# Four weight sums moved from ScalarE to VectorE in a cross-attention and feed-forward kernel

## The reference

```python
def attention(ctx, latents, mask):            # latents = layernorm(x)
    xn, ln = layernorm(ctx), layernorm(latents)
    q = ln @ W_q                               # 4 heads of 64
    k, v = split(concat([xn @ W_kv, ln @ W_kv]))
    sim = (rmsnorm(q) * 64**-0.5) @ rmsnorm(k).T
    return softmax(where(mask, sim, -max)) @ v @ W_out + b_out

def bit_linear(x, w):                          # both sides quantized
    sx = 127 / clip(max|x| over the row, 1e-5);   xq = clip(round(x * sx), -128, 127) / sx
    sw = 1 / clip(mean(|w|), 1e-5);               wq = clip(round(w * sw), -1, 1) / sw
    return xq @ wq.T

x = x + attention(ctx, layernorm(x), mask)
h = bit_linear(layernorm(x), w1)               # 256 -> 1024
h = silu(depthwise_conv3_over_tokens(h) + conv_b)
x = x + bit_linear(h, w2)                      # 1024 -> 256
```

## Time and profile before

| | us |
|---|---|
| median of 3 runs | 440.35 (440.3 to 441.3) |
| profiled execution, its own time | 440.35 |
| its span, first to last instruction | 438.5 |
| TensorE busy | 407.9 (93%) |
| VectorE busy | 379.5 (87%) |
| ScalarE busy | 314.4 (72%) |

### The profile page before, as it was taken

How to read it: one execution, slowest core, us unless ns; L and a number is a source line. 1 busy time by engine, 2 the same in 40 slices (tenths; PEclk the granted TensorE clock), 3 DMA queues, 4 the chain that set the end, 5 groups by cost and what they waited for, 6 DMA issues and landing times.

```text
span 438.5 us, 14218 instructions
## 1 busy us (share of the span) xinstructions
PE 407.9 (93%) x5918; PEld 276.6 (63%) x5918; DVE 379.5 (87%) x611; ACT 314.4 (72%) x368; POOL 84.3 (19%) x119
## 2 busy tenths in 40 slices
PE   1999997699999999999999999999999987899976
PEld 1666675466766676666666666676666744576764
DVE  4789999987887889879879879879879899999995
ACT  2456777479988756757766766667766688999985
POOL 2175564860000120010120010111001010212110
PEclk9999999999999999999999999999999996999999
DMA  7802000611111111111201111111101000000102
GB/s 212 227 2 72 1 1 1 225 44 63 49 51 48 53 40 50 62 37 39 73 30 48 61 39 50 63 39 37 51 25 51 5 0 4 0 27 25 50 24 73
DMA packets 27588, 22.53 MB, mean 51 GB/s; under 512 B 7232, under 2 KB 27268, under 8 KB 27524
## 3 DMA queue, kind: packets, MB, share of 16 engines
q1 hardware_dynamic: 26112, 21.59, 15.2%
q10 hardware_dynamic: 1412, 0.01, 0.2%
HBM read 6.91 MB, written 2.10 MB: 21 GB/s over the span
## 4 chain that ended last, share of the span: by engine, by line
PE 54%; DVE 25%; ACT 12%; issue 5%; DMA 3%; ACTq 0%; SPq 0%; POOL 0%; DVEq 0%; POOLq 0%
DVE arena L719 14%; PE sc L1633 13%; PE heads L1650 6%; PE heads L1651 5%; PE heads L1652 5%; PE heads L1459 4%; ACT arena L1259 3%; PE sc L1470 3%; ACT qq L1350 2%; PE by L1538 2%; PE sc L1739 2%; DMA kst<-kk 2%; ACT qq L1358 2%; PE bx L1470 2%; PE by L1470 2%
## 5 line engine op out<-in xcount | busy, mean ns | idle before, releaser
L719 DVE SCALAR_TENSOR_TENSOR arena<-arena 128x1024 bf16<-128x1024 f32 x160 | 192.9, 1237 | 32.5 <-ACT arena L1259 32.3
L1259 ACT ACTIVATE arena<-sc,kb 128x1024 f32<-128x1024 f32 x160 | 169.8, 1114 | 70.6 <-PE sc L1633 70.6
L1650 PEld LDWEIGHTS heads<-v,arena 128*128 128x128 bf16 x1280 | 117.0, 97 | 39.1 <-issue 26.7
L1650 PE MATMUL heads<-v,arena 128*128 128x65 f16 x1280 | 130.6, 194 | 3.2 <-DVE arena L719 1.4
L1651 PE MATMUL heads<-v,arena 128*128 128x64 f16 x1280 | 129.6, 195 | 0.0
L1652 PE MATMUL heads<-v,arena 128*128 128x65 f16 x1280 | 129.0, 192 | 0.0
L1633 PE MATMUL sc<-qs,kst 64*128 64x512 f16 x960 | 117.9, 378 | 3.4 <-DVE kk L661 1.6
L1651 PEld LDWEIGHTS heads<-v,arena 128*128 128x128 bf16 x1280 | 118.8, 97 | 0.1
L1652 PEld LDWEIGHTS heads<-v,arena 128*128 128x128 bf16 x1280 | 118.8, 99 | 0.0
L1633 PEld LDWEIGHTS sc<-qs,kst 64*128 64x128 f16 x960 | 40.1, 94 | 49.3 <-issue 5.0
L497 POOL TENSOR_TENSOR ss<-ss,halves 128x16 f32<-128x16 f32 (+1 forms) x10 | 27.4, 2738 | 24.6 <-DVE ss L639 24.6
(11 more groups left out here) (215 smaller groups left out, 602.0 us busy)
## 6 DMA issues: line engine op xcount, KB each, us to landing
kst<-kk SPq DMA_DIRECT2D x80, 128.0 KB, 2.0
xs<-in_x SPq DMA_DIRECT2D x8, 256.0 KB, 5.4
qs<-qq SPq DMA_DIRECT2D x16, 128.0 KB, 2.0
out<-cbuf SPq DMA_DIRECT2D x7, 256.0 KB, 2.1
xs<-in_ctx SPq DMA_DIRECT2D x6, 256.0 KB, 5.4
xs<-in_L_ffn_w SPq DMA_DIRECT2D x1, 1024.0 KB, 6.1
cbuf<-in_L_ffn_w SPq DMA_DIRECT2D x1, 1024.0 KB, 8.2
arena<-in_L_xattn_W_kv SPq DMA_DIRECT2D x2, 256.0 KB, 5.2
```

What stands on the lines that cost most here:

```text
L719: e.scalar_tensor_tensor(out=rest[:, j, :, :], in0=prob[:, j, :, :], scalar=SHRINK, in1=probh[:, j, :, :], op0=ALU.mult, op1=ALU.subtract) ...
L1259: a_.activation(prob[:, j, :, :], sc[(j + 1) % 2][:, :, :], ACT.Exp, bias=kb[:, bass.ds(i * QUAD + j, 1)]).then_inc(exp_done[j], 1)
L1650: t_.matmul(o, hi, row[:, 0:OW], start=first and sub == 0, stop=False, skip_group_check=True)
```

## The change

The four sums leave ScalarE's stream and go into VectorE's, as a reduction with absolute values over the same four halves. They need no output array now, so `sizes` goes. In ScalarE's stream the exponentials of quads 0 to 4 become one loop. In VectorE's stream each of the quads 2, 3 and 4 has one sum after its first remainder, and quad 4 another after its third. The waits for earlier sums go; the wait for the loads stays.

```diff
-        sizes = arena[:, xd0 + 5 * P * 4:xd0 + 5 * P * 4 + HID * D // P // 2]
@@ VectorE
+            def weights_summed(n):
+
+                dve.wait_ge(s["w_ffn"], 32)
+                half = (w1raw, w2raw)[n // 2][:, n % 2 * (HID * D // P // 2):(n % 2 + 1) * (HID * D // P // 2)]
+                e.tensor_reduce(wsum[:, n:n + 1], half, AX.X, ALU.add, apply_absolute_value=True).then_inc(s["wabs_ready"], 1)
@@ first_two_units
-                over(1, nq, remainders)
+                over(1, nq - 3, remainders)
+                for q in range(3):
+                    remainder(nq - 3 + q, 0)
+                    weights_summed(q)
+                    remainder(nq - 3 + q, 1)
+                    remainder(nq - 3 + q, 2)
+                    if q == 2:
+                        weights_summed(3)
+                    remainder(nq - 3 + q, 3)
@@ ScalarE
-            def weights_summed(n):
-
-                act.wait_ge(s["w_ffn"], 32)
-                wait(act, "wabs_ready", n)
-                half = (w1raw, w2raw)[n // 2][:, n % 2 * (HID * D // P // 2):(n % 2 + 1) * (HID * D // P // 2)]
-                a_.activation(sizes, half, ACT.Abs, accum_out=wsum[:, n:n + 1]).then_inc(s["wabs_ready"], 1)
-
-            with act.Fori(0, nq - 3) as i:
+            with act.Fori(0, nq) as i:
                 exponentials(i, i)
-            exponentials(nq - 3, nq - 3)
-            weights_summed(0)
-            exponential(nq - 2, nq - 2, 0)
...
-            weights_summed(3)
-            exponential(nq - 1, nq - 1, 2)
-            exponential(nq - 1, nq - 1, 3)
```

## The result

| | before | changed |
|---|---|---|
| median, 7 runs each | 441.12 us (440.3 to 441.4) | 443.54 us (442.61 to 444.76) |
| profiled execution, its time | 440.35 | 445.12 |
| its span | 438.5 | 443.3 |

The changed kernel is slower. The ratio over all executions of the first comparison (27 of the changed kernel, median 444.31 us) is 1.0073, with a 95% interval of 1.0057 to 1.0089. Two later comparisons gave 1.0050 (1.0034 to 1.0066) and 1.0060 (1.0042 to 1.0079). The forecast of 442.5 us had the direction and the place of the cost, but the time of the 27 executions lies 1.8 us above it, and above its range, which ended at 443.6.

What follows compares the result with a forecast made beforehand. The prediction took TensorE to bound the stretch with the sums. Four stalls of 0.72, 0.50, 0.50 and 0.44 us, together 2.16, with 0 for ScalarE's relief, were added to 440.35 us, giving 442.5 us, range 441.0 to 443.6.

Steps and rivals of the forecast that it cites:

- What bounds the stretch: From 87 to 112 us TensorE alone sets the pace, busy 25.00 of 25.00 us; VectorE and ScalarE are off the path.
- What leaves ScalarE: Removing ScalarE's four 1.05 us activations and merging its loop gains 0, between -0.2 and +0.2 us, as TensorE never waited.
- What one sum costs: A sum on VectorE delays the next instruction's start by 1.14 us, with bounds of 0.60 and 1.35 us.
- The upper bound: A VectorE sum costs at most 1.35 us, if stretched like the remainder that runs 1.44 us instead of 1.23.
- The stalls: TensorE waits four times for a delayed remainder: 0.72 us in quad 2, 0.50 in quad 3, 0.50 and 0.44 in quad 4.
- the formula: Second remainder ready 4.53 us after a pair's scores start, wanted at 5.17; slack 0.64, so a 1.14 us sum stalls 0.50.
- What is behind the sums: After the first unit's last values nothing gets narrower or swallows the delay; the 2.16 us reach the end.
- The time: The profiled execution's 440.35 us plus 2.16 us of stalls gives 442.5 us.
- The range: Execution time from 441.0 us, towards half-price sums with part of the stalls left, to 443.6 us for stretched sums.
- The rival of the clock: Stalls let TensorE's clock fall for one 6 us stretch, costing up to 6 us more, up to 448.5 us; chance 0.02.

Runs made afterwards that it cites:

- a_nosums: The changed kernel with the four sums left out, wsum set to a constant; ratio 1.0006 to the kernel before.
- a_both: The changed kernel with ScalarE also keeping its four activations, their sums unread; ratio 1.0073 to the kernel before, on 4 executions.
- a_again: The changed kernel unaltered, run and profiled again; median 443.71 us, ratio 1.0050 to the kernel before.
- b_round: The kernel before with the weights' rounding moved from ScalarE to VectorE and the second clipping behind quad 8; median 440.36 us, ratio 0.9969.
- b_one: The kernel before with one of its four sums on VectorE, between the first two remainders of quad 3; ratio 1.0013.
- a_hot: The changed kernel with 36 extra matmuls at four places in TensorE's waits before quad 1; ratio 1.0080 to the kernel before.
- a_spread: The changed kernel with one sum in each of quads 1 to 4, behind a pair's second remainder; ratio 1.0018 to the kernel before.
- a_warm: The changed kernel with five extra 128x512 matmuls at one place in TensorE's waits before quad 1; ratio 1.0048 to the kernel before.
- b_hot: The kernel before with 36 extra matmuls at four places in TensorE's waits before quad 1; ratio 1.0032 to the kernel before.
- a_thin: The changed kernel with each sum over 512 numbers instead of 1024; ratio 1.0005 to the kernel before.
- b_again: The kernel before unaltered, run again for a second profile; ratio 0.9999, span 439.6 us.
- a_again2: The changed kernel unaltered, run a third time; ratio 1.0060 to the kernel before.

## Why the prediction was right or wrong

**What bounds the stretch**: right. Where a sum adds time, TensorE idles by it, and without sums (a_nosums) the middle is 20.93 us to the last digit.

**What leaves ScalarE, priced at 0**: right. a_nosums and a_both differ from their bases by nothing in the middle.

**What one sum costs, 1.14 us in starts**: right; 1.13 measured. The reduction in quad 2 was not lengthened, though it began beside GpSimd's last instruction. The upper bound was taken from one stretched remainder of 1.44 us; the same trace has one of 1.69 us beside GpSimd (at 91.05), so it was no bound for that kind of stretch.

**The stalls**, against a_again (distances between scores, before and after, each with the shift up to the scores of quad 2, 0.09 us, taken off):

| | predicted | measured shift | idle time shown |
|---|---|---|---|
| quad 2 | 0.72 | 0.85 | 0.68 |
| quad 3 | 0.50 | 0.60 | 0.43 |
| quad 4, first pair | 0.50 | 0.60 | 0.43 |
| quad 4, second pair | 0.44 | 0.43 | 0.24 |
| sum | 2.16 | 2.48 | 1.78 |

Place, order and releaser of each were as forecast. The first three are some 0.1 us larger than the formula: the values block was ready at the computed moment, but it was wanted 0.1 us earlier than I had put it. The shift is 0.17 to 0.19 us more than the idle time shown, because the block before it runs out first: its matmuls take 0.91 us from first start to last end, while without a stall the next block starts 0.75 us after it began. In the last pair two errors of mine cancel: its block was wanted 0.1 us earlier for the same reason, and 0.1 us later because the stall before it was longer than I had put it. So the agreement of 0.43 with 0.44 is partly luck. In the first profile the first stall was 0.60 instead of 0.85, since the low clock had let GpSimd's work end before the sum.

**What is behind the sums, priced at nothing**: right as far as the attention goes, and open behind it. The six units after the first take 202.7 to 202.8 us in every profile, with and without sums (b_round alone has less, 201.5). The part to the end is 326.6 to 328.0 us over all profiles, and all of that variation arises in one place. Counted from the end of the seventh unit, ScalarE's instructions in all 14 profiles lie within 0.1 us of one another up to 51 us, and from 59 us on they are shifted by an amount that stays. Around that place lies the low clock after the attention. What remains behind the seventh unit is 124.1 to 124.3 us where the low clock begins 47.6 to 48.2 us behind it and lasts 6.8 us (before, b_one, a_hot, a_spread, a_warm), 124.7 to 125.3 where it begins at 49.5 to 50.7 (a_both, a_nosums, b_hot, b_round, changed, a_thin), and 124.2, 124.7 and 124.7 where it begins at 52.1 to 52.4 and lasts 3.4 us (b_again, a_again, a_again2). The first two groups hold kernels with and without sums, b_hot and a_hot even the other way round. But the four profiles of the changed kernel's full work without extra matmuls (changed, a_again, a_again2, a_both) have 327.4 to 327.9 us to the end, the two of the kernel before 326.9. Whether shifting the work by 2.4 us makes the longer case likelier was not tried.

**The time**: this is the step that failed. I added 2.16 us to 440.35, "the median of the runs shown as well". Three executions were no measure of the kernel's time. Run beside the changed kernel it had a median of 441.12 us, and 441.4 in the later series (72 executions, 440.3 to 443.1), and the profiled execution was one of its fastest: no low clock ahead of quad 2, a short start, the shortest kind of end. Of the 1.8 us between 442.5 and 444.31, this base is 0.8 (441.12 against 440.35). Another 0.3 is the sum of the stalls, 2.48 us in a_again where I had 2.16. The last 0.7 us is in neither; by the profiles it lies in the parts ahead of the sums and behind them, where I had put the change's effect at nothing, and its cause stays open. From 441.4 us the same step gives 443.6, against medians of 443.71 and 444.15 in the two later sets. The range was built from the uncertain cost of a sum and left no room for the base, nor for the parts around.

**The rival of the clock**: the low clock is real, at 3.4 us and a cost of 1.7 us (1.9 in a_nosums), but not by the stalls. It begins before the first of them, it appears in a kernel without sums (a_nosums), and no profile has it in the middle part, where TensorE was busy 21.43 of 23.20 us (a_again):

```profile
91.00:114.20 23.20, 21.43 (x422) 14.44 (x418) 21.44 (x19) 14.83 (x14) 3.55 (x3) 1.00 0.17 54
```

The first comparison, 1.0073 or 3.2 us, exceeds the middle part's 2.2 to 2.5 us; the other two, 2.2 and 2.6 us, agree with it. That the first set merely caught more of the slow starts and ends explains this only in part, for the mean clock recorded with each execution says more. Of the changed kernel's 39 executions in the three sets, the 16 with a mean clock of 0.995 or 0.996 took 443.6 us on average, the 11 with 0.991 or 0.992 took 444.6. Of the 72 of the kernel before in the later series, the 21 with the higher clock took 441.7 and the 29 with the lower 441.1. (The rest, below 0.99, average 444.2 and 441.5.) So the kernels are 2.0 us apart in the one group and 3.5 in the other, and 2.7 us over all their executions. One reading is that the changed kernel's low-clock stretches fall more often where they cost much, ahead of quad 2 or late behind the attention. The executions without a profile do not say where theirs fall, so whether the change brings that about, and how, stays open.

## What to carry to other kernels

Before an instruction is put into the stream of an engine that is not the bound, compute for that very slot when its successor is ready and when it is wanted; 0.70 us of free time per pair did not help a sum of 1.14 us in the middle of a pair with 0.64 us of slack, while behind the pair it was free in a_spread's quads 2 to 4, clear of GpSimd. An engine with more idle time in the mean (ScalarE here) may be loaded to the brim where nothing waits for it, and starve others elsewhere: move the work at the place where the bounding engine idles, not the work that is hidden. And take the base of a forecast from many executions: cut the profile into parts, and ask of each outer part how it varies.

## What the runs showed of the hardware

- A reduction beside GpSimd. In a_spread the sum at 90.81 kept its 1.21 us while GpSimd worked, and the remainders after it were stretched, to 1.68 us at the most. In the kernel before, the 132 remainders without a GpSimd instruction beside them took 1.20 to 1.23 us, and those beside one up to 1.69. GpSimd's own timeline shows the other side: its addition that began beside the sum took 0.66 us, the next one, beside remainders, 1.53. In the first profile of the changed kernel both took 0.66, with VectorE idle beside them but for the last 0.1 us.

```profile
91.67 0.66 POOL L546 TENSOR_TENSOR bparts<-bparts 3x256 f16<-3x256 f16 x1
92.41 1.53 POOL L547 TENSOR_TENSOR bparts<-bparts 3x256 f16<-3x256 f16 x1
```

  The remainder reads two operands out of SBUF, the sum one. The Trainium skill, "SBUF — State Buffer", section "Who interferes with whom", says that a VectorE instruction with two SBUF inputs contends with a GpSimd instruction that reads SBUF, and that a tensor_reduce on this chip never does. By that rule this was to be expected, and this trace agrees.
- The start of the kernel varies by 2 us (74.4 to 76.4 us to the first scores), and a load can be a part of it. In a_spread, the latest, the bias of the context's layernorm landed 7.4 us after its issue instead of 6.7, and ScalarE's first gains, which waited for it, began at 9.76 us; in the kernel before they waited for TensorE and began at 9.13. Those 0.6 us are less than half of the 1.5 us by which a_spread is late at the first scores. The waits of ScalarE up to 22 us in a_spread:

```profile
ACT arena L1201 <- DMA lng<-in_L_xattn_ln_x_b: 5.4, 1, 5.4
```

- Nearly the same TensorE activity can leave the clock at 1.00 or bring it to 0.50. In the 9 us that begin 1.15 us behind the first scores TensorE was busy 5.20 us in the kernel before and 5.13 in b_again, where the clock stayed, and 5.05 in the changed kernel and 4.94 in a_nosums, where it fell from about 86 us on and the part up to quad 2 grew to 17.52 and 17.74 us. Whether so small a difference decides, or something else, no run here shows.
